# Causal mask of the transposed scores by TensorE in every batch, group 0's tokens by GpSimd, layer norm statistics dealt over steps

## What is computed

```python
def attn_a(x):                                  # layer A, 16 heads of 8 channels
    scores = einsum('bhqd,bhkd->bhqk', q, k) / sqrt(8)
    mask = triu(full((t, t), -max), k=1)        # key after query: out
    return (softmax(scores + mask) @ v) @ wo + bo

def ffn(x):                                     # 8 experts, hidden 512
    vals, idx = top_k(x @ Wr, 2)
    w = softmax(vals)
    return sum(w * ((silu(x @ Wg[e]) * (x @ Wu[e])) @ Wd[e]) * 12 ** -0.5 for e in idx)

x = x + attn_a(layernorm(x))
x = x + ffn(layernorm(x))
x = x + attn_b(layernorm(x))                    # layer B, no mask
x = x + ffn(layernorm(x))
```

## Time and profile before

| | us |
|---|---|
| median of 3 runs (1163.05 to 1168.38) | 1166.69 |
| the profiled execution, own time | 1166.68 |
| its span, first to last instruction | 1164.9 |
| TensorE busy | 1029.9 (88%) |
| VectorE busy | 755.5 (65%) |
| ScalarE busy | 672.4 (58%) |
| GpSimd busy | 525.5 (45%) |

### The profile page before, as it was taken

The page is one execution under the profiler, slowest core; times in us unless marked ns, Lnnn a source line. Parts: engine busy times, 40 slices in busy tenths (PEclk is TensorE's granted clock), DMA queues, the critical chain, the costliest instruction groups (busy, mean ns, idle before and its releaser), DMA issues.

```text
span 1164.9 us, 28879 instructions
## 1 busy us (share of the span) xinstructions
PE 1029.9 (88%) x9290; PEld 716.6 (62%) x9290; DVE 755.5 (65%) x2322; ACT 672.4 (58%) x1399; POOL 525.5 (45%) x980
## 2 busy tenths in 40 slices
PE   2998999897989999999798979999888799999990
PEld 1444555453468989999443434444443589999990
DVE  4687778877777333456777888888877663334442
ACT  2365676663644545556277858897757445455550
POOL 2243444332742610344687736455736436004455
PEclk9998999996989999999778979998888899999995
DMA  6446544562235878887544323343221469778873
GB/s 152 104 114 138 116 110 99 151 181 57 54 118 174 271 233 236 260 255 236 125 111 104 101 56 85 89 107 84 65 49 44 130 191 280 227 242 256 272 225 109
DMA packets 201723, 175.03 MB, mean 150 GB/s; under 512 B 19812, under 2 KB 160616, under 8 KB 201576
## 3 DMA queue, kind: packets, MB, share of 16 engines
q1 hardware_dynamic: 193384, 156.41, 49.1%
q0 software_dynamic: 8192, 16.79, 4.8%
HBM read 122.99 MB, written 50.14 MB: 149 GB/s over the span
## 4 chain that ended last, share of the span: by engine, by line
PE 60%; DVE 11%; issue 6%; POOL 5%; DMA 4%; SPq 3%; ACT 1%; POOLq 0%; ACTq 0%; DVEq 0%
PE psS L1358 9%; PE psT L1365 9%; PE psO L321 8%; PE psS L355 7%; PE psO L1381 4%; PE psN L1381 4%; DVE mx L671 4%; PE psS L386 3%; PE psT L363 3%; POOL xn L1259 3%; PE psM L276 2%; PE psN L328 2%; DMA eo<-ysb 2%; PE psN L337 1%; PE psM L1346 1%
## 5 line engine op out<-in xcount | busy, mean ns | idle before, releaser
L671 DVE TENSOR_REDUCE mx<-psS 128x3 f32<-128x384 f32 (+1 forms) x512 | 311.4, 617 | 119.5 <-PE psS L386 61.8
L355 PE MATMUL psS<-kst,qst 48*128 48x256 bf16 (+1 forms) x1024 | 201.7, 286 | 46.4 <-DVE mx L671 33.2
L558 ACT ACTIVATE pT<-psT,scb 128x512 f32<-128x512 f32 x256 | 193.9, 777 | 43.2 <-PE psT L363 40.7
L363 PE MATMUL psT<-qst,kst 50*128 50x256 bf16 (+1 forms) x1024 | 194.7, 278 | 4.6 <-DMA qst<-scr_m 2.2
L1422 DVE TENSOR_TENSOR hT<-sg,psT 128x512 f32<-128x512 f32 x142 | 97.5, 686 | 154.4 <-PE psT L1365 127.7
L1245 POOL DMA_INDIRECT xg<-xn,slot x128 | 123.1, 962 | 131.3 <-DVE ysb L1417 72.1
L1358 PE MATMUL psS<-xTt,wgc 128*128 128x128 f32 x1136 | 153.7, 279 | 5.7 <-issue 5.3
L355 PEld LDWEIGHTS psS<-kst,qst 48*128 48x128 bf16 x1024 | 66.2, 97 | 146.0 <-DVE mx L671 68.2
L1365 PE MATMUL psT<-xTt,wuc 128*128 128x128 f32 x1136 | 152.2, 278 | 1.5 <-DMA wuc<-in_L_ffn_Wu 1.4
L790 POOL TENSOR_SCALAR_AFFINE_SELECT pT<-pT 128x256 f32<-128x256 f32 x224 | 90.6, 412 | 133.0 <-ACT pT L553 131.8
L553 ACT ACTIVATE pT<-psT 128x384 f32<-128x384 f32 x256 | 122.9, 490 | 46.1 <-PE psT L363 35.9
(11 more groups left out here) (225 smaller groups left out, 1595.1 us busy)
## 6 DMA issues: line engine op xcount, KB each, us to landing
wgc<-in_L_ffn_Wg SPq DMA_DIRECT2D x142, 256.0 KB, 3.1
wuc<-in_L_ffn_Wu SPq DMA_DIRECT2D x142, 256.0 KB
scr_part<-part SPq DMA_DIRECT2D x128, 128.0 KB, 2.1
qst<-scr_part SPq DMA_DIRECT2D x64, 192.0 KB, 3.7
kst<-scr_part SPq DMA_DIRECT2D x64, 192.0 KB, 4.7
xin<-xg SPq DMA_DIRECT2D x142, 64.0 KB
eo<-ysb SPq DMA_DIRECT2D x142, 64.0 KB
scr_part<-part SPq DMA_DIRECT2D x32, 192.0 KB, 1.9
```

The costliest lines, as they stand in the source:

```text
L355: return nc.tensor.matmul(ps[:, c0:c0 + n], q_[r64, t, q0], k_[r64, t, 0:n], start=(half == 0), stop=True, skip_group_check=True)
L363: return nc.tensor.matmul(ps[:, c0:c0 + T - q0], k_[m64, t, half * P:half * P + P], q_[m64, t, q0:T], start=(half == 0 or not L.causal), s ...
L558: nc.scalar.activation(pT[:, g % 8, 0:cols], psT[g % 2][:, 0:cols], ACT.Exp, scale=scb[r][:, 0, i:i + 1], bias=scb[r][:, 1, i:i + 1]).then ...
L671: nc.vector.tensor_reduce(mx3[:, u, 0:n, pos:pos + 1].rearrange("p a b -> p (a b)"), psS[h % 2][:, 0:kcols(L)].rearrange("p (a k) -> p a k ...
```

## The change

`MASKED` becomes 0: TensorE masks the transposed scores in all 16 batches, and GpSimd's selects go. Group 0's tokens in layer A are made by GpSimd in step 14, one behind each head. The statistics are dealt over two steps each: in layer A from step 5 to steps 4 and 5, and from 13 to 12 and 13; in layer B from step 7 to two halves in steps 6 and 7 and in 9 and 10, and from step 14 to 13 and 14. The fourth combining of layer B goes from step 7 to step 8. `ffn_over` no longer waits for the stores.

```diff
-MASKED = B - 2
+MASKED = 0
         def ffn_over(eng, l):
             eng.wait_ge(f_sem["y"], TILES * (l + 1))
-            for i in range(2):
-                eng.wait_ge(f_st[i], tiles_done(i, l, TILES))
...
         def pool_beside(l):
+                if l == 0 and j == 14 and h > 0:
+                    k = h - 1
+                    if k == 0:
+                        pool.wait_ge(s_ln[0], 1)
+                    nc.gpsimd.tensor_scalar(xn[:, k, :], x[:, k, :], mean_rstd[:, k, 0:1], mean_rstd[:, k, 1:2],
+                                            ALU.subtract, ALU.mult).then_inc(r_sem["xn"], 1)
...
         def dve_beside(l):
-                if l == 0 and j == 5 and h == 0:
+                if l == 0 and j == 4 and h == 0:
                     dve.wait_ge(s_xlast, 16)
-                if l == 0 and j == 5:
-                    dve_ln_at(dve, h, HALF, HALF, s_lnA, 3)
+                if l == 0 and j == 4 and h % 2 == 0:
+                    dve_ln_at(dve, h // 2, HALF, HALF, s_lnA, 3)
+                if l == 0 and j == 5 and h < 3:
+                    dve_ln_at(dve, HALF // 2 + h, HALF, HALF, s_lnA, 3)
...
-                if l == 1 and (j, h) in ((4, 4), (5, 4), (6, 4), (7, 2)):
-                    dve_combine_1(dve, 0, j - 4)
+                if l == 1 and (j, h) in ((4, 4), (5, 4), (6, 4), (8, 4)):
+                    dve_combine_1(dve, 0, min(j - 4, 3))
...
-                if l == 1 and j == 7:
-                    dve_ln_at(dve, h, SIZE[0], SIZE[1], s_lnB, 3)
-                if l == 0 and j == 13:
-                    if h == 0:
-                        dve.wait_ge(x1, HALF)
-                    dve_ln_at(dve, h, 0, HALF, s_ln[0], 1)
-                if l == 0 and j == 14:
-                    if h % 4 == 1:
-                        dve_tokens(dve, 0, h - 1, h + 3)
+                for part, (first, times) in enumerate(((6, 3), (9, 4))):
+                    lo, count = SIZE[0] + part * SIZE[1] // 2, SIZE[1] // 2
+                    if l == 1 and j == first and h % 4 == 0:
+                        dve_ln_at(dve, h // 4, lo, count, s_lnB, times)
+                    if l == 1 and j == first + 1 and h < 3:
+                        dve_ln_at(dve, count // 2 + h, lo, count, s_lnB, times)
+                if l == 0 and j == 12 and h == 0:
+                    dve.wait_ge(x1, HALF)
+                if l == 0 and j == 12 and h % 2 == 0:
+                    dve_ln_at(dve, h // 2, 0, HALF, s_ln[0], 1)
+                if l == 0 and j == 13 and h < 3:
+                    dve_ln_at(dve, HALF // 2 + h, 0, HALF, s_ln[0], 1)
...
-                if l == 1 and j == 14:
-                    if h == 0:
-                        dve.wait_ge(x1, SIZE[0])
-                    dve_ln_at(dve, h, 0, SIZE[0], s_ln[2], 1)
+                if l == 1 and j == 13 and h == 0:
+                    dve.wait_ge(x1, SIZE[0])
+                if l == 1 and j == 13 and h % 2 == 0:
+                    dve_ln_at(dve, h // 2, 0, SIZE[0], s_ln[2], 1)
+                if l == 1 and j == 14 and h < 3:
+                    dve_ln_at(dve, SIZE[0] // 2 + h, 0, SIZE[0], s_ln[2], 1)
```

## The result

| | before | after |
|---|---|---|
| median of 4 runs each, us | 1165.59 (1163.05 to 1168.38) | 1183.35 (1182.1 to 1186.8) |
| ratio, 95% interval | 1 | 1.0167 [1.0141, 1.0192] |
| span of the profiled execution, us | 1164.9 | 1181.3 |

What follows compares the result with a forecast made beforehand. It took TensorE to bound layer A's steady step; +21.0 - 1.0 + 1.4 - 1.4 + 3.5 + 1.0 - 1.9 = +22.6, less 1.0 for steps 15 and 16, on 1166.68 gave 1188.3 us; two in ten left out, 1171 to 1198.

Steps and rivals of the forecast that it cites:

- The forecast case: Whole kernel: slower by 21 us, at 1188.3 us, its own range 1177 to 1197; chance 0.73.
- Masks, +21.0: Layer A, steps 3 to 16: one added TensorE matmul per head costs 1.5 us a step, 14 steps, +21.0 us.
- No zeroing, -1.0: Layer A: without GpSimd's selects VectorE's split L627 may give time back, -1.0 us, between 0 and -1.4.
- Steps 15 and 16, -1.0: Layer A, steps 15 and 16: masks lie partly beside waits for the routing, -1.0 us.
- Statistics and tokens in layer A, +1.4 and -1.4: Statistics add 0.7 us to each of steps 4 and 12; normalisations leaving VectorE for GpSimd save 1.4 in step 14.
- Layer B's halves, +3.5: Layer B, steps 6 to 10: two roots at 6 us each, combining and statistics, 14.9 us for 11.4, +3.5.
- Group 2's statistics, +1.0: Layer B: statistics go from step 14 to 13, root at head 2 of 14; +1.0 us (-2 to +2).
- Start of layer B, -1.9: Start of layer B: the store's wait goes, the copy ysb is next, -1.9 us (0 to -1.9).
- (a): Both layers: the clock stays up behind the stalls, a root costs its bare 3 us; 1167.4 us, chance 0.10.
- (b): Both layers: dealing the statistics removes the root's stalls, so the kernel gets faster, 1150 us; chance 0.04.
- (c): Layer A: TensorE's idle and queued time hides the masks, steady step 15.9 us, whole 1167 us; chance 0.05.
- (d): Added root and combining in step 8 bring longer half clock, masks cost twice there; 1200 us, chance 0.08.

Runs made afterwards that it cites:

- e5: The changed kernel with GpSimd's 224 selects put back on a tile that nothing reads, masks still by TensorE; ratio 1.0181 to the kernel before.
- e1: The kernel before with the masks of the transposed scores moved to TensorE in all batches and nothing else; ratio 1.0124, +14.4 us.
- e6: The kernel before without the wait for the stores ahead of layer B; ratio 0.9977, not told apart from no change.
- e2: The changed kernel with GpSimd zeroing batches 0 to 13 as before, all else of the change kept; ratio 1.0054 to the kernel before, +6.3 us.
- e7: The kernel before with layer B's statistics of blocks 16 to 31 in two halves and the fourth combining in step 8; ratio 1.0037, +4.3 us.
- e10: The changed kernel with the zero fill of the experts' input moved from steps 13 and 14 to steps 8 to 11; ratio 1.0139 to the kernel before.
- e3: The changed kernel with the root's 13 instructions dealt one behind each of heads 2 to 14, in both layers; 1166.85 us, ratio 1.0012 to the kernel before.
- e4: e3 with GpSimd zeroing batches 0 to 13 again; 1158.37 us, ratio 0.9953 to the kernel before.
- e8: e4 with group 0's tokens back on VectorE, four at each of heads 1, 5, 9 and 13 of step 14; ratio 0.993 to the kernel before.

## Why the prediction was right, step by step

The forecast case held: slower, by the masks, with the stalls still there. The time came out 5 us under 1188.3 and inside the case's own range. By its own terms:

**Masks, +21.0.** The place was right, and so was the price of a head, 0.12 us (0.60 against 0.48). A steady step grew by 1.22 us net of what the missing selects gave back, for 20.0 / 14 = 1.43 forecast; with the selects running (e5) by 1.46 for 1.5. Of the prediction's two prices the one from the whole of step 17 was the better: it gave 17.02 us for a steady step, which then took 17.10, while 1.5 was taken nearer to the sum by heads. What failed is the count of the steps that pay: the prediction let only 0.3 us of the masks hide beside the stalls, and left even these out of its 14 x 1.5. In e1 the four steps with and behind a root gained 1.6 us instead of 4.9, so 3.3 us did not show there, beside waits or in a shorter half clock. With ten steps at 1.22 and this 1.6, 13.8 us come out; the trace of e1 has 13.75 more up to the first tile.

**No zeroing, -1.0.** Too small, by e5: 0.24 us a step, 14 steps, 3.4 us, and by the split's own duration against the earlier trace rows 0.14 and 2.0 us. The prediction gave 1.4 as the most. The kernel before can't show the effect by itself, since each of its steps from 3 to 18 has selects or masks. The Trainium skill, GPSIMD Engine Reference, section 8 (Key points), says that GpSimd contends with VectorE instructions of two SBUF inputs; the trace agrees in kind (L627: 682 ns without selects, 820 and 921 with them), and that section gives no size.

**Steps 15 and 16, -1.0.** Wrong: from step 15 to the first tile e1 is 3.0 us longer, not less than two steady steps' 2.4. The routing's waits hid nothing.

So the masks alone in layer A: forecast 21.0 - 1.0 - 1.0 = 19.0, measured 13.75. Of the 5.25 between them, 2.9 is the net price of a steady step (14 x 0.21) and 3.3 what did not show in the stall steps, less the 1.0 that steps 15 and 16 did not give: 5.2.

**Statistics and tokens in layer A, +1.4 and -1.4.** The price of the statistics was right to the tenth: after's steps 4 and 12 are 17.85 and 17.78 us for e1's 17.17 and 17.09, +0.7 each. What came back is less clear. As after less e1 the sum is -2.5. Of this -1.7 lie in step 3, in which the two kernels have the same queues, so that part is spread and not the change; steps 5, 6, 13 and 14 give -0.9 and the stretch from step 15 on -1.2. TensorE waits for none of GpSimd's tokens in step 14, as forecast; 16 of them at 0.79 us are 12.7 us for 12.5. How much the tokens gave was not tried.

**Layer B's halves, +3.5.** Measured +4.4: the three kernels without them (before, e1, e6) average 100.8 for steps 6 to 10 (101.5, 99.0 and 101.9), the five with them (after, e2, e5, e7, e10) average 105.2. After has 106.4. The root's price of 6 was right in B: steps 7 and 10 lie 6.9 and 5.6 over their neighbours' 17.55. The spread among kernels that don't differ here, 99.0 to 101.9, is of the size of the term's error. Part of it is the bound: GpSimd's addition at the start of step 6 lies up to 3.1 us further behind VectorE's normalisation in some traces than in others. Counted from the normalisation (L583) the averages are 101.7 and 106.5, so +4.8. What makes the rest of the spread is open.

**Group 2's statistics, +1.0.** Measured -0.5.

**Start of layer B, -1.9.** The wait fell by 1.92, from 3.76 to 1.84, with the copy ysb behind it, as said. But steps 0 and 1, which end with this wait, took only 0.7 us less, and e6's total can't be told from no change.

**The rivals.** (a) is out as it stands: after the stall in step 5 the clock is at 0.50. But its mechanism may be there in part, with the masks alone (e1) and with the whole change: in layer A's four stall steps 8.5 us of clock were missing before, 5.1 in e1 and 3.4 after. These steps lie 11.3 us over steady ones now (79.7 less four times 17.10) where 15.4 were; how much of that is the shorter low clock and how much masks that lie beside a wait was not told apart. (b) is out: one wait of 2.4 us in steps 5 and 13 (just under the 2.5 that was named as the sign), 2.5 in steps 7 and 10, 2.6 in step 14 of B. It was right about what decides: e3, in which the stalls go, wins 16.5 us over the changed kernel. It was wrong about how much: in layer A nothing with the masks by TensorE, since a DMA is next, and 4.6 of 15.4 us with GpSimd's (e4). (c) is out: 17.10, not 15.88. (d) did not come: the added root in step 10 cost 5.6, not its dear end, and the total stayed below the forecast.

**Together:** layer A +11.3 for 19.0, the rest +5.1 for 2.6, in sum +16.4 for 21.6. The forecast was high because it let too little of the masks hide in the stall steps, and took too little back for the selects; behind the first tile 2.5 us more were lost than forecast, 1.4 of them in steps 6 to 10. That the total came within 5 us is in part luck: layer A was forecast 7.7 us too high and the rest 2.5 too low.

## What to carry to other kernels

Work moved to the engine on the path costs most of its time there, however idle the engine that gave it up was: here 1.46 us a step at most, of 16 x 0.12 = 1.9. What comes back is the contention that it caused where it was (here at most 0.24 us a step), and some of it in steps that stall anyway. A chain of small dependent instructions on an in-order engine is to be dealt out one link at a time, not shortened in number around it: dealing the statistics into two halves, each with a root, doubled the stalls of layer B's steps 7 to 10. And before removing a stall, look for the transfer that it covers: here a small DMA took over in layer A, and moving the large one beside it moved the collision. Last, a step that is bounded by one engine's instruction moves when that engine is late: take the bound on a second engine before a gain is looked for in the wrong step.

## What the runs showed that was not expected

GpSimd's selects of 128x256 stretch VectorE's two-input operation of 128x512 from 682 ns to 820 and 921 ns, though each works on its own tile. The traces show that it is a wait for the whole select and not a slower rate. Before, then e5:

```profile
147.14 0.41 POOL L790 TENSOR_SCALAR_AFFINE_SELECT pT<-pT 128x256 f32<-128x256 f32 x1 [0.69 <-ACT pT L553]
147.27 0.82 DVE L627 TENSOR_TENSOR part<-rest,part 128x512 bf16<-128x512 f32 x1
...
155.68 0.41 POOL L792 TENSOR_SCALAR_AFFINE_SELECT idle<-idle 128x256 f32<-128x256 f32 x1 [1.17 <-ACT pT L554]
155.71 0.92 DVE L628 TENSOR_TENSOR part<-rest,part 128x512 bf16<-128x512 f32 x1
```

In both the split ends 0.54 us after the select does, and so it does in all 23 places of the two traces where a select that was already running reached more than 0.15 us into it (0.540 to 0.544 us). The select of before started 0.13 us ahead of the split and that of e5 0.03, which is the whole difference between 820 and 921 ns. The other way round it holds too: the four selects that started inside a split ended 0.265 or 0.266 us after it, and took up to 0.87 us for their 0.41.

A DMA of a few rows, on which TensorE waits, kept it waiting for 1.4 us (e3's step 6), 2.2 (e3's step 14) and 2.5 (e8's step 14) once the root's stall no longer covered it, in steps where the DMA engines were busy for 0.57, 0.74 and 0.69 of the time. The share alone doesn't decide: e8's step 13, at 0.70, has no such wait. In e3 TensorE's clock stands at 0.50 behind it (250 to 252 us) as behind a stall of VectorE; in e8's step 14 it stayed at 1.00.

At the start of the kernel the column of the granted clock can't be taken at its word. Before's stretch from 32.65 to 34.57 us says 1.00, while the group of four projections that fills it takes 1.92 us, and in step 8 such a group takes 1.13. The trace has no record of the clock before 53 us, and the column then says 1.00:

```profile
32.65:34.57 1.92, 1.92 (x6) 1.09 (x6) 0.60 (x2) 0.00 (x0) 0.00 (x0) 1.00 0.76 190
```

```profile
32.65 1.92 PE L276 MATMUL psM<-xT,w_permA 128*128 128x256 f32 x4
...
137.68 1.13 PE L276 MATMUL psM<-xT,w_permA 128*128 128x256 f32 x4
```
